# Experts' gathered rows turned by four SBUF-to-SBUF transfers and one 32x32 block transposition on VectorE in place of four TensorE transpositions

## The reference

```
x = x + layernorm(attention(layernorm(x)))          # 16 heads of 32, latent 128, extra rotary-like part
x = x + layernorm(ffn(layernorm(x)))

ffn(h):  scores = sigmoid(h @ router)               # 16 experts, 2 are chosen for each token
         h1     = h @ w_up[e]                       # 512 -> 256, for the chosen experts
         a      = relu(h1)^2 * combine
         routed = a @ w_down[e]                     # 256 -> 512
         shared = relu(h @ shared_up)^2 @ shared_down
         return routed + shared
```

## Time and profile before

| | us |
|---|---|
| median of three runs | 1658.06 |
| the profiled execution | 1658.72 |
| its span, first to last instruction | 1656.9 |
| TensorE busy | 1569.0 (95%) |
| VectorE busy | 926.2 (56%) |
| ScalarE busy | 829.9 (50%) |
| GpSimd busy | 799.4 (48%) |

### The profile page before, as it was taken

The page is one execution under the profiler, slowest core; times in us unless marked ns, Lnnn a source line. Parts: engine busy times, 40 slices in busy tenths (PEclk is TensorE's granted clock), DMA queues, the critical chain, the costliest instruction groups (busy, mean ns, idle before and its releaser), DMA issues.

```text
span 1656.9 us, 22215 instructions
## 1 busy us (share of the span) xinstructions
PE 1569.0 (95%) x7386; PEld 1079.2 (65%) x7386; DVE 926.2 (56%) x1896; ACT 829.9 (50%) x1496; POOL 799.4 (48%) x820
## 2 busy tenths in 40 slices
PE   4799999999999999999998999998999999979997
PEld 3465656656566566565644778886666666657886
DVE  3566767666676767766673515482111111129998
ACT  2355566565665656656464444312333333355554
POOL 1167697776967769777695310002222222133341
PEclk9799999999999999999999999997999999989999
DMA  4757278383684745846643042127533434387673
GB/s 118 208 141 201 80 195 256 102 237 113 189 248 113 213 140 169 255 116 195 194 152 128 24 184 79 51 102 253 205 128 131 130 129 129 106 283 239 221 242 133
DMA packets 123767, 270.57 MB, mean 163 GB/s; under 512 B 15396, under 2 KB 27044, under 8 KB 117508
## 3 DMA queue, kind: packets, MB, share of 16 engines
q1 hardware_dynamic: 97256, 205.97, 41.3%
q0 software_dynamic: 12912, 41.82, 8.0%
q10 hardware_dynamic: 13488, 21.37, 3.5%
HBM read 154.03 MB, written 92.01 MB: 149 GB/s over the span
## 4 chain that ended last, share of the span: by engine, by line
PE 82%; DMA 7%; ACT 2%; DVE 2%; SPq 2%; issue 2%; POOL 1%; DVEq 0%; ACTq 0%; POOLq 0%
PE bank L109 13%; PE bank L699 10%; PE bank L677 9%; PE bank L755 8%; PE bank L778 8%; PE bank L598 7%; PE bank L584 6%; PE bank L603 6%; PE bank L614 6%; DMA a<-kq_scratch 4%; PE bank L738 2%; PE bank L623 2%; SPq L1729 2%; PE bank L727 1%; DMA kq_scratch<-a 1%
## 5 line engine op out<-in xcount | busy, mean ns | idle before, releaser
L1570 POOL TENSOR_TENSOR a<-a 128x512 f32<-128x512 f32 x384 | 496.0, 1320 | 153.1 <-ACT a L1373 92.9
L1373 ACT ACTIVATE a<-bank 128x512 f32<-128x512 f32 x512 | 297.5, 598 | 245.9 <-PE bank L603 198.7
L888 DVE TENSOR_REDUCE a<-bank 128x1 f32<-128x512 f32 x512 | 323.6, 681 | 54.6 <-PE bank L584 53.5
L109 PE MATMUL bank<-a 128*128 128x512 f32 (+1 forms) x864 | 240.6, 402 | 6.2 <-DVE a L834 4.0
L598 PE MATMUL bank<-a 128*128 128x512 f32 x512 | 221.9, 433 | 2.9 <-ACT a L1373 2.3
L603 PE MATMUL bank<-a 68*128 68x512 f32 x512 | 205.7, 402 | 1.3 <-ACT a L1363 0.2
L677 PE MATMUL bank<-c 128*128 128x512 f32 x768 | 188.9, 406 | 18.5 <-ACT c L1425 11.6
L584 PE MATMUL bank<-a 128*128 128x512 f32 x512 | 181.8, 428 | 21.6 <-DMA a<-kq_scratch 21.2
L1639 POOL DMA_INDIRECT f<-h_scratch,f x79 | 74.8, 947 | 252.5 <-PE bank L738 229.5
L109 PEld LDWEIGHTS bank<-a 128*128 128x128 f32 (+1 forms) x864 | 161.1, 189 | 52.9 <-issue 10.3
L677 PEld LDWEIGHTS bank<-c 128*128 128x128 f32 x768 | 149.1, 196 | 56.2 <-issue 12.4
(11 more groups left out here) (186 smaller groups left out, 1891.3 us busy)
## 6 DMA issues: line engine op xcount, KB each, us to landing
a<-kq_scratch SPq DMA_DIRECT2D x192, 256.0 KB, 5.7
kq_scratch<-a SPq DMA_DIRECT2D x32, 1024.0 KB, 4.1
a<-a SPq DMA_DIRECT2D x80, 256.0 KB, 5.4
yp_scratch<-f ACTq DMA_DIRECT2D x79, 256.0 KB, 2.0
a<-in_L_attn_x SPq DMA_DIRECT2D x15, 1024.0 KB, 8.9
x_scratch<-a SPq DMA_DIRECT2D x8, 1024.0 KB, 4.9
h_scratch<-a SPq DMA_DIRECT2D x8, 1024.0 KB, 12.9
hT_scratch<-s SPq DMA_DIRECT2D x8, 1024.0 KB, 6.0
```

Source lines behind the costliest of these rows:

```text
L109: t = e.matmul(out, a[n], b[n], start=n == 0 and m == 0, stop=n == len(ah) - 1 and m == 2)
L888: e.tensor_reduce(K.mx[:, i, j:j + 1], K.MX[n % 3][:], AX.X, ALU.max).then_inc(Z.max, 1)
L1373: e.activation(K.pt[:, n % NP, :], K.SC[n % 2][:], ACT.Exp, scale=SCALE).then_inc(Z.exp, 1)
L1570: e.tensor_tensor(K.acc[:, j, :], a, K.pt[:, n % NP, :], ALU.add).then_inc(Z.acc, 1)
```

## The change

The turn of a tile leaves TensorE. A transposition in VectorE turns blocks of 32x32 in place only, so a block must first be brought to the 32 partitions that it is to end on. ScalarE issues four DMAs for a tile (`move`), each of which copies 128 columns of `K.ht` (128 partitions, 512 bytes of each) to 32 partitions of a new buffer `K.hx` (four rows of 512 bytes side by side on each). Then one VectorE instruction turns the 64 blocks of the tile into `K.hTt`. The order of features and of rows that results from this is made up for outside the loop: w_up's rows are permuted on the host before the launch, and the constant `c_row`, by which rows get their places in a tile, is permuted too; because of that the tile numbers, which were read from `c_row`, now come from a constant of their own (`K.count`). `K.hx` takes the place of `K.fhT[:, 0]`, which overlaps `K.raw`, so the load of h for batch FIRST moves from `split h` into `reload`, behind the last turn. Four semaphores of constants are merged into one (`set_done`).

The diff, without the merged semaphores' waits and the declarations of names:

```diff
 def experts_order():
-    out = [("fetch", i) for i in range(4)]
+    out = [("fetch", i) for i in range(4)] + [("move", 0), ("move", 1)]
     for i in range(NTILE + 3):
         if i < NTILE:
             out.append(("e turn", i))
             if i + 4 < NTILE:
                 out.append(("fetch", i + 4))
+            if i + 2 < NTILE:
+                out.append(("move", i + 2))
...
 def expert_room(K):
     room = K.fhT[:, 1], K.faT
     K.ht = room[0]
+    K.hx = K.fhT[:, 0]
...
 # tensor_program
-    def e_turn(i):
-        z = i % 2
-        w.wait_ge(Z.ht[i % 4], 16 * (i // 4 + 1))
-        if i >= 2:
-            w.wait_ge(Z.hTt, i - 1)
-        else:
-            w.wait_ge(Z.prefix, 1)
-        for k in range(4):
-            t = e.transpose(K.TR[z][:, k * P:(k + 1) * P], K.ht[:, i % 4, k * P:(k + 1) * P], K.ident[:])
-        t.then_inc(Z.eT, 1)
...
 # vector_program
-            e.tensor_scalar(K.space[:, at + P:at + P + NTILE], K.row[:, 0:NTILE], q[:, t:t + 1], K.tok[:, t:t + 1],
+            e.tensor_scalar(K.space[:, at + P:at + P + NTILE], K.count, q[:, t:t + 1], K.tok[:, t:t + 1],
...
+    def e_turn(i):
+        z = i % 2
+        w.wait_ge(Z.hx[i % 4], 16 * 4 * (i // 4 + 1))
+        if i >= 2:
+            w.wait_ge(Z.eu, i - 1)
+        else:
+            w.wait_ge(Z.dn, 4 * FIRST)
+        e.transpose(K.hTt[:, z, :].rearrange("p (k i r) -> p k i r", k=4, r=HD),
+                    K.hx[:, i % 4, :].rearrange("p (i k c) -> p k i c", k=4, c=HD)).then_inc(Z.hTt, 1)
...
 # scalar_program
-    def e_turn(i):
-        z = i % 2
-        w.wait_ge(Z.eT, i + 1)
-        if i >= 2:
-            w.wait_ge(Z.eu, i - 1)
-        else:
-            w.wait_ge(Z.dn, 4 * FIRST)
-        e.copy(K.hTt[:, z, :], K.TR[z][:]).then_inc(Z.hTt, 1)
+    def move(i):
+        n = i % 4
+        w.wait_ge(Z.ht[n], 16 * (i // 4 + 1))
+        if i >= 4:
+            w.wait_ge(Z.hTt, i - 3)
+        for q in range(4):
+            e.dma_start(K.hx[HD * q:HD * q + HD, n, :], K.ht[:, n, q * P:(q + 1) * P]).then_inc(Z.hx[n], 16)
...
 # gpsimd_program, fetch
-            w.wait_ge(Z.eT, i - 3)
+            w.wait_ge(Z.hx[i % 4], 16 * 4 * (i // 4))
...
 # sync_program
     def split_h(b):
-        if b + 1 < B:
+        if b + 1 < B and b + 1 != FIRST:
...
+        e.dma_start(K.count, ins["c_tid"][0:NTILE].partition_broadcast(P)).then_inc(Z.tok, 16)
...
     def reload():
+        w.wait_ge(Z.h_lo, 4 * FIRST)
+        w.wait_ge(Z.hTs, 16 * (FIRST + 1))
+        w.wait_ge(Z.hTt, NTILE)
+        e.dma_start(K.raw, K.hT_d[FIRST]).then_inc(Z.hT, 16)
         w.wait_ge(Z.ed, NTILE)
...
 # constants and inputs
-        "c_row": np.arange(P, dtype=np.float32),
+        "c_row": np.arange(P, dtype=np.float32).reshape(4, HD).T.reshape(P).copy(),
...
+    given["L0_ffn_w_up"] = np.ascontiguousarray(given["L0_ffn_w_up"].reshape(E, 4, 4, HD, FI).swapaxes(1, 2).reshape(E, D, FI))
```

More of the change, by code:

```diff
@@ L344, in __init__ @@
         self.full, self.free = many("ms_full", 2), many("ms_free", 2)
-        self.ones, self.small, self.sel, self.rope = make("ones_set"), make("dve_step"), make("sel_set"), make("rope_done")
+        self.set, self.small, self.sel, self.rope = make("set_done"), make("dve_step"), make("sel_set"), make("rope_done")
         self.var = {k: make(f"var_{k}") for k in KINDS}
         self.off = {k: make(f"off_{k}") for k in KINDS}
-        self.half, self.root = make("half_set"), make("root_step")
+        self.root = make("root_step")
         self.dT = make("dT_done")
@@ L360, in __init__ @@
         self.ew, self.tok, self.cc = many("ew_in", 6), make("tok_in"), make("cc_in")
-        self.onesf, self.sig, self.A, self.totals, self.choice = (make(n) for n in ("onesf_set", "sig_done", "A_done", "totals_full", "choose_step"))
+        self.sig, self.A, self.totals, self.choice = (make(n) for n in ("sig_done", "A_done", "totals_full", "choose_step"))
         self.te, self.prefix, self.slots = make("te_done"), make("prefix_done"), make("slots_done")
         self.pair, self.inv, self.idx = make("pair_done"), make("inv_done"), make("idx_done")
-        self.ht, self.yps = many("ht_in", 4), many("yp_out", 7)
-        self.eT, self.hTt, self.eu, self.ear, self.eav, self.eT2, self.eaT, self.ed, self.yo = (make(n) for n in (
-            "eT_full", "hTt_done", "eu_full", "e_relu", "e_square", "eT2_full", "eaT_done", "ed_full", "yo_done"))
+        self.ht, self.hx, self.yps = many("ht_in", 4), many("hx_in", 4), many("yp_out", 7)
+        self.hTt, self.eu, self.ear, self.eav, self.eT2, self.eaT, self.ed, self.yo = (make(n) for n in (
+            "hTt_done", "eu_full", "e_relu", "e_square", "eT2_full", "eaT_done", "ed_full", "yo_done"))
         self.su2, self.sd2 = many("su2_in", 4), make("sd2_in")
@@ L448, in ffn_room @@
     K.row = tile([P, P])
+    K.count = tile([P, NTILE])
     K.slots = [(tile([P, NT]), tile([P, NT])) for _ in range(2)]
@@ L619, in total @@
         bank = begin("total", u)
-        w.wait_ge(Z.ones, 1)
+        w.wait_ge(Z.set, 1)
         for j in range(4):
@@ L783, in tensor_program @@
               "values": values, "total": total, "project": project, "turn2": turn2, "route": route, "fold": fold, "up": up,
-              "down": down, "choose late": lambda n: choose(0), "invert rows": spread, "e turn": e_turn, "e up": e_up, "e turn2": e_turn2,
+              "down": down, "choose late": lambda n: choose(0), "invert rows": spread, "e up": e_up, "e turn2": e_turn2,
               "e down": e_down}
@@ L1194, in spread @@
             w.wait_ge(Z.slots, 2)
-            w.wait_ge(Z.tok, 2 * 16)
+            w.wait_ge(Z.tok, 3 * 16)
             if n >= DEEP:
@@ L1272, in vector_program @@
               "choose early": lambda n: advance("early", n), "choose late": lambda n: advance("late", n), "invert rows": spread,
-              "index": index, "e up": e_up, "e turn2": e_turn2, "add": add, "rescale": rescale, "finish": finish}
+              "index": index, "e turn": e_turn, "e up": e_up, "e turn2": e_turn2, "add": add, "rescale": rescale, "finish": finish}
     for name, *at in K.order:
@@ L1537, in scalar_program @@
               "turn2": turn2, "route": route, "split h": split_h, "split up": split_up, "round up": round_up,
-              "round down": round_down, "up": up, "store": store, "choose early": choose, "e turn": e_turn, "e up": e_up,
+              "round down": round_down, "up": up, "store": store, "choose early": choose, "move": move, "e up": e_up,
               "e down": e_down, "take": take, "rescale": rescale, "finish": finish}
@@ L1554, in gpsimd_program @@
     e.dma_start(K.pe[HD:, :], ins["c_pe"]).then_inc(Z.w1b, 16)
-    e.memset(K.ones[:], 1.0).then_inc(Z.ones, 1)
-    e.memset(K.mhalf, -0.5).then_inc(Z.half, 1)
+    e.memset(K.ones[:], 1.0).then_inc(Z.set, 1)
+    e.memset(K.mhalf, -0.5).then_inc(Z.set, 1)
     chain = Steps(Z.root)
@@ L1586, in root @@
         w.wait_ge(Z.root, chain.n)
-        w.wait_ge(Z.half, 1)
+        w.wait_ge(Z.set, 2)
         e.tensor_tensor(r, ve, K.mhalf, ALU.pow).then_inc(*chain.next())
@@ L1625, in choose @@
             w.wait_ge(Z.hTs, 16 * B)
-            e.memset(K.onesf, 1.0).then_inc(Z.onesf, 1)
+            e.memset(K.onesf, 1.0).then_inc(Z.set, 1)
         early[0] += 1
```

2 lines of the change are left out of this document (1 added, 1 removed).

## The result

The kernel became slower. After the change the median is 1669.63 us (7 runs, 1667.88 to 1677.06), against 1661.70 (7 runs, 1656.63 to 1663.43) for the kernel before on the same chip: the ratio is 1.0058, with a 95% interval of 1.0042 to 1.0075. Forecast was 1651. The profiled execution took 1667.88 us, its span is 1665.7.

What follows compares the result with a forecast made beforehand. TensorE bounds the experts' stage at 4.11 us a tile; after the change ScalarE would, at 3.95. The sum: 1658.7 - 9.8 (stage's gain) + 2.5 (weights) = 1651.4, forecast 1651 us, range 1628 to 1692.

Steps and rivals of the forecast that it cites:

- up to relu 11, without the weights: Start of the experts' stage: relu 0 waits behind four groups of moves, relu 3 at 1149.80, then 3.95 us a tile.
- weights beside it: Early tiles' moves beside weight loads in full DMA engines: cost between nothing and 10 us, taken as 2.5.
- relu 11 to 75, ScalarE's round: Steady part: four issues of 0.64 us plus 1.37 make ScalarE's round 3.95 us, against 4.11 now.
- relu 75 to the last copy: Stage's end, after the last moves: relu and square 0.9, then TensorE's 12.9 us; last down ends at 1448.0.
- behind it, h's load: Stage's end: h for batch FIRST loads behind the last turn; cost nothing, a few us if its cover were gone.
- the upper bound of 10: Highest weights' cost: four issues of 1 us for five tiles, less 0.64 each, is 7, plus late gathers.
- The start's order: Moves of tiles 0 to 3 queue ahead of relu 0, at 1139.99; up 0 begins 2.1 us later, at 1134.6.
- a step of 0.67: Time from issue to issue in ScalarE's queue at which the gain is gone; 0.64 was taken.
- TensorE as the bound with cheap issues: First rival, experts' stage: ScalarE's issues cost 0.37 to 0.57 us, so TensorE's 3.67 us round holds; 1629 us; 18%.
- Moves that stall in the queue at 0.80 each: Second rival, ScalarE's queue: step 0.80 us, round 4.59, 0.48 longer than now; 1701 us; 28%.
- The third rival: Nothing to measure: the step is 0.66 or so, or the weights cost 8 us; 1657 us; 12%.
- the 0.3 us that TensorE waits in each round: Sign in TensorE's rows: a gap of about 0.3 us before turn2, waiting for VectorE's square and behind it ScalarE.

Runs made afterwards that it cites:

- sp_moves: Changed kernel with moves issued by SyncE (SP) instead of ScalarE, last nine experts' weights between them in rounds 1 to 8: 1644.11 us, ratio 0.9935 to before.
- act_weights: Moves on SP's queue, the nine experts' weights issued by ScalarE, one expert a round in rounds 1 to 8: 1646.72 us, ratio 0.9920 to before.
- both: The turn stays on TensorE and its copy on ScalarE as before, and ScalarE issues four moves a tile that nothing reads: 1671.56 us.
- no_weights: Changed kernel without the weight loads of the last nine experts, whose tiles use the seventh's weights: 1658.17 us.
- small_moves: Changed kernel with each move from the fifth tile on carrying 128 instead of 512 bytes of a partition, as many issues: 1664.74 us.

## Why the prediction was wrong

It forecast 1651 us with 48% on faster, and the kernel became 0.6% slower. The measured time lies in the range, and the direction had 31%. By its own steps:

| step of the sum, us against before | forecast | measured |
|---|---|---|
| up to relu 11, without the weights | +3.6 | +5.3 |
| weights beside it | +2.5 | +11.2 |
| relu 11 to 75, ScalarE's round | -9.8 | -7.2 |
| relu 75 to the last copy | -3.7 | -3.1 |
| behind it, h's load | 0 | +0.2 |
| sum (of the unrounded terms) | -7.3 | +6.4 |

(The forecast of the first row is the prediction's relu 3, 1149.80, and eight rounds of 3.95, behind the cast at 1125.79: 55.6, where it was 52.0. The 9.8 of the third row happens to be the same number as the prediction's whole gain: 64 x 4.103 - 64 x 3.95.) The measured sum stands beside 9.2 us between the profiled executions, of which 2.5 arise ahead of the stage, and beside 7.0 to 12.5 that the interval of the ratio gives; a us or so is open.

**The step that failed** is "I take 2.5, near the lower end, since the last weight load is issued at 1159.6". It was 11.2, above even the upper bound of 10. I had priced the queue: so many issues of 1 us instead of 0.64. The issues stayed at 2.5 to 2.6 us for four in all rounds from the fifth tile on. What grew were the landings: 8.8 to 11.2 us from a tile's last issue to the transposition that waited for it, where 5.8 lie between them in the steady part (median of tiles 20 to 70). With them grew the waits for `hx` and for free places of `ht`, which the prediction called met with times from a stage in which the DMA engines had room ("a 64 KB copy lands in 2.2 us when the queue is free and 7.0 at most"). The row that said otherwise stood in the prediction: a share of 1.06 at 384 GB/s in the earlier trace rows. Read as a budget, it comes near the loss: each tile brings 0.26 MB more, the 14 tiles moved by relu 11 bring 3.7 MB. At the 384 GB/s of that row this is an estimate of 9.6 us, which could have been made before. The windows show 4.0 MB more, which at the 291 GB/s of the kernel after is 13.7 us, beside 11.2 for the weights and 16.5 in all. And the date 1159.6 was one of the kernel before; in full engines SP's issues last up to 5.25 us and the last goes out at 1172.46, 44.2 us behind the cast where it was 33.8.

**The start's order** was mis-sized by 1.7 us (5.3 for 3.6). Relu 0 came 4.4 us later for a forecast of 3.7. The first up began 11.4 us behind the cast for a forecast of 8.8: the first tile's transposition came 3.8 us behind its last issue, where 2.2 had been taken. ScalarE's first sixteen issues take 10.74 us from 1132.15, 0.67 each, and TensorE idles 11.43 us ahead of the first up; its granted clock is 0.85 in the mean of 1140 to 1160, where it was 1.00.

**The round** was right as a steady value, 3.94 for 3.95, and by the reason given: ScalarE's queue with the four issues. That it fits to 0.01 us is partly luck: relu, copy and store take 1.31 us for a forecast of 1.37 (the copy starts 0.28 us behind the relu's start), and from the first issue to the relu it is 2.63 for 2.58. An issue lasts 0.624 us, and 0.64 from start to start in the mean. Missing were the longer rounds, worth 2.6 of 9.8 us. The prediction had seen that the gain is gone from a step of 0.67 on; the step wasn't the cause, but a margin of 0.03 us left nothing to pay another cost with.

**The rivals.** TensorE as the bound with cheap issues (1629) needed a step of 0.57 or less; it is refuted by the 0.64 and by the gap-free 3.66 of `sp_moves`, which shows what it would have been. Moves that stall in the queue at 0.80 each (1701) didn't come. The third rival (12%), in which the weights cost 8 us and the time stays at 1657, named the term that failed and still put it too low. A page of the Trainium skill (DMA: Bandwidth & Descriptors, "Issuing engines are not separate DMA queues") calls the sequencer's time usually small. In this kernel it is 2.5 us of a round of 3.94, and moving it to another queue (with the weights put between the moves) is the difference between 0.6% slower and 0.7% faster. In the other sense of the section's title the runs agree with it: a second queue for the weights gave little or no bandwidth, 319 GB/s against 307 between 1140 and 1200 us (`act_weights`, `sp_moves`) and 318 against 320 with the weights spread.

**Right as forecast:** VectorE's transposition (0.701 for 0.71), TensorE's round of 3.66 when nothing else binds, the DMA share of the steady part (0.66 for 62%), moves landed in time there, and h's load at no cost. No row shows a cost of the merged semaphores, the constant or the permuted w_up. One sign was placed wrongly: the 0.3 us that TensorE waits in each round were forecast before turn2, as a gap; they lie around down, and only the distances of the starts show them.

**Open:** why rounds with 16 KB packets of instructions are longer; how much of the DMA engines' time the number of the pieces takes and how much their bytes; and a us or so of the difference of the medians.

## What to carry to other kernels

Moving work from a bound engine to DMAs has two prices, the issue in a queue and the bytes; look up each where it is scarcest, the issue in the queue of the engine that would be the next bound, the bytes in the stretch where the DMA share is already 1. Where that share is full, count MB and divide by the GB/s of the row, as a lower bound if the new pieces are smaller; waits taken from a quiet stretch don't hold there, and pacing mostly moves them. Put such DMAs on the queue of an engine that is far from the bound: here that was SP's, with the weights put between the moves, and it made 1.0058 into 0.9935.

## What the runs showed of the hardware

- An SBUF-to-SBUF DMA of 64 KB in 512-byte pieces costs ScalarE's queue 0.624 us (kernel after) and SP's 0.603 (`sp_moves`; medians of 316), a store of 256 KB to HBM 0.33.
- A copy of 0.59 us on ScalarE runs while its queue issues DMAs (1242.04 and 1242.12 in `both`).
- Full DMA engines moved 384 GB/s with gathers, stores and weights (share 1.06), and 293 to 332 with the 512-byte moves among them (in the windows 1140 to 1160 and 1160 to 1200 us with a share of 1.00 to 1.10, kernels with whole moves and all weights).
- From a tile's last issue to the transposition that waited for it, it took 8.8 to 11.2 us while the DMA engines were full (kernel after, 1140 to 1200 us), and 2.2 and 4.0 us without the last weights (`no_weights`, the first two tiles).
- A move's four issues took 3.99 us instead of 2.54 when a 16 KB packet of instructions was moved beside them (`no_weights`, 1312.88); in that run and `small_moves` all 17 issues over 0.75 us after 1200 us have such a packet beside them. The cause isn't shown.
